# A decoder layer on one core: Q's bias ahead of the exponentials on ScalarE, and the turned probabilities ahead of the tail's transposes on TensorE

## The reference

```
q, k, v = x @ Wq + bq, x @ Wk + bk, x @ Wv + bv      # 16 query heads, 4 key/value heads, 128 wide
q, k    = rope(q), rope(k)
x = layernorm(x + softmax(causal(q @ k.T / sqrt(16))) @ v @ Wo + bo)
x = layernorm(x + wkv(w, u, k=x, v=context))         # a decaying maximum and two decaying sums over the 256 rows
x = layernorm(x + x @ W.T + bias + low_rank_experts(x))   # the 2 best of 16 experts for each row
```

## Time and profile before

| what | value |
|---|---|
| median of 3 runs | 1581.77 us (1580.96 to 1586.83) |
| the profiled execution, its own time | 1579.19 us |
| its span, first to last instruction | 1577.4 us |
| granted TensorE clock, mean | 0.992 |
| busy: PE, PEld, DVE, ACT, POOL | 97%, 89%, 84%, 71%, 64% |

### The profile page before, as it was taken

One profiled execution on the slowest core, in us unless ns is written; L12 is line 12 of the kernel. 1 busy time (PEld: TensorE's weight loads), 2 busy tenths in 40 slices (PEclk: granted clock), 3 DMA queues, 4 the chain that ended last, 5 costly groups with the idle time before them and its releaser, 6 DMA issues.

```text
span 1577.4 us, 32696 instructions
## 1 busy us (share of the span) xinstructions
PE 1534.2 (97%) x10492; PEld 1396.1 (89%) x10492; DVE 1326.1 (84%) x3435; ACT 1117.8 (71%) x2995; POOL 1005.0 (64%) x853
## 2 busy tenths in 40 slices
PE   8999999999999999999999999999999988989998
PEld 7899999999999999999999999999899977878786
DVE  6776688889889888898898989898989897877964
ACT  6877787877787878787878787878787865234333
POOL 2555586757676767676767667676767563644644
PEclk9999999999999999999999999999999998999999
DMA  7776444424441444244424441445144522112121
GB/s 245 243 256 209 156 144 141 129 67 152 148 144 50 154 153 141 62 154 154 141 61 149 142 159 48 125 151 180 48 128 154 167 65 97 58 68 94 60 89 54
DMA packets 81641, 202.62 MB, mean 128 GB/s; under 512 B 10432, under 2 KB 11072, under 8 KB 81472
## 3 DMA queue, kind: packets, MB, share of 16 engines
q1 hardware_dynamic: 81472, 200.53, 40.3%
HBM read 120.80 MB, written 37.75 MB: 101 GB/s over the span
## 4 chain that ended last, share of the span: by engine, by line
PE 81%; DVE 9%; issue 3%; POOL 2%; ACT 2%; DMA 1%; DVEq 1%; SPq 0%; POOLq 0%; ACTq 0%
PE bank L546 24%; PE bank L548 23%; PE bank L547 23%; PE bank L670 5%; PE bank L615 2%; DVE ED L1366 1%; PE bank L616 1%; PE bank L653 1%; PE bank L661 1%; DVE PS L1325 1%; DMA SW<-QB 1%; PE bank L685 1%; DVE OTl L1269 1%; ACT Xh L768 0%; DVE RO L1280 0%
## 5 line engine op out<-in xcount | busy, mean ns | idle before, releaser
L546 PE MATMUL bank<-Xh,W 128*128 128x256 f32 x1280 | 357.4, 279 | 3.6 <-DVE Vl L1242 1.5
L548 PE MATMUL bank<-Xh,W 128*128 128x256 f32 x1280 | 356.2, 278 | 0.0
L547 PE MATMUL bank<-Xl,W 128*128 128x256 f32 x1280 | 355.8, 278 | 0.0
L1050 POOL TENSOR_TENSOR Ql<-RC,Qh 128x512 fp32r<-128x512 f32 x127 | 168.8, 1329 | 191.9 <-ACT Qh L768 191.7
L783 ACT ACTIVATE S<-S,NM 128x128 f32<-128x128 f32 (+1 forms) x512 | 229.0, 450 | 68.7 <-DVE NM L1181 67.7
L1038 POOL TENSOR_TENSOR SW<-SW,tables 128x512 f32<-128x512 f32 x128 | 175.4, 1370 | 125.0 <-DMA SW<-QB 125.0
L546 PEld LDWEIGHTS bank<-Xh,W 128*128 128x128 f32 x1280 | 241.5, 189 | 5.5 <-issue 2.8
L548 PEld LDWEIGHTS bank<-Xh,W 128*128 128x128 f32 x1280 | 241.2, 188 | 0.0
L547 PEld LDWEIGHTS bank<-Xl,W 128*128 128x128 f32 x1280 | 241.0, 188 | 0.0
L768 ACT ACTIVATE PTh<-bank 128x384 fp32r<-128x384 f32 x256 | 125.1, 489 | 148.7 <-PE bank L670 147.6
L768 ACT ACTIVATE S<-S,RL 128x128 f32<-128x128 f32 (+1 forms) x512 | 204.4, 450 | 31.7 <-DVE RL L1188 31.3
(11 more groups left out here) (161 smaller groups left out, 4428.1 us busy)
## 6 DMA issues: line engine op xcount, KB each, us to landing
W<-kept SPq DMA_DIRECT2D x140, 512.0 KB, 4.5
SW<-QB SPq DMA_DIRECT2D x256, 128.0 KB, 2.3
kept<-W SPq DMA_DIRECT2D x40, 512.0 KB, 4.8
XR<-XR SPq DMA_DIRECT2D x64, 128.0 KB, 2.3
RO<-in_xn SPq DMA_DIRECT2D x16, 512.0 KB, 4.0
KVT<-in_ctxt SPq DMA_DIRECT2D x16, 512.0 KB, 4.8
mixed<-RO SPq DMA_DIRECT2D x16, 512.0 KB, 4.5
XR<-in_xt SPq DMA_DIRECT2D x15, 512.0 KB, 4.2
```

What stands on the lines that cost most here:

```text
L546: nc.tensor.matmul(dst, lhs[0], rhs[0], start=first, stop=False)
L547: nc.tensor.matmul(dst, lhs[0], rhs[1], start=False, stop=False)
L548: return nc.tensor.matmul(dst, lhs[1], rhs[0], start=False, stop=last)
L1050: gp.tensor_tensor(Q[1][:, :, :], RC[:, i % 2, :, :], Q[0][:, :, :], ALU.subtract).then_inc(q_lo, 1)
```

## The change

Two calls are moved, one on each of two engines. No instruction is added or taken away.

On TensorE, the turning of the probabilities moves ahead of the tail's transposes. This matters only in the slots that have a piece of the tail: four of every sixteen.

On ScalarE, in odd slots, `before_rotation(n)` moves ahead of `exponentials(n)`. Even slots are as they were.

```diff
@@ TensorE, slot(n), behind the output projection
+                g = head_of(n, L_T)
+                if g is not None:
+                    pe.wait_ge(normed, g + 1)
+                    above(pe, pt_lo, g)
+                    if g == 0:
+                        pe.wait_ge(const_in, 16)
+                    for k in range(3):
+                        last = nc.tensor.transpose(pt_ps[:, k * P:(k + 1) * P], S[:, g % 2, k * P:(k + 1) * P], Ident[:, :])
+                    last.then_inc(turned, 1)
                 for t in range(TT):
                     tau = tail_of(n, T_TURN + t)
...
                         last.then_inc(y_turned, 1)
-                g = head_of(n, L_T)
-                if g is not None:
-                    pe.wait_ge(normed, g + 1)
...
-                    last.then_inc(turned, 1)
@@ ScalarE, odd(n)
                 tail(n, 0)
+                before_rotation(n)
                 exponentials(n)
-                before_rotation(n)
                 extras(n)
                 x_high(n)
```

## The result

| | median | range of runs |
|---|---|---|
| before | 1580.96 us | 1579.02 to 1586.83, 7 runs |
| changed | 1572.34 us | 1571.93 to 1574.44, 6 of 7 runs |

The ratio is 0.9945 with an interval of 0.9934 to 0.9956. That is 8.6 us less, and under the low end of the range, 1574. In a second series of five rounds the changed kernel took 1573.47 us against 1580.91, ratio 0.995 (0.9937 to 0.9963). The seventh run of the changed kernel, the profiled one, was disturbed (1886 us at a granted clock of 0.75), so I read two later profiles, with spans of 1570.2 us both.

The account below looks back on a forecast made before the run. TensorE was taken as the bound, busy 1167.82 of 1170 us from 100 to 1270 us. Savings of 2.2 + 0.2 = 2.4 us took the median 1581.77 us to 1579.4 us; range 1574 to 1585 us.

Parts of the forecast that it names:

- the ceiling: TensorE, 100 to 1270 us: busy 1167.82 of 1170 us, so other engines' order can give back at most 2.2 us.
- the four stalls: TensorE's second half of `y` (L661) waits four times for VectorE's sum L1377: 2.3 us together, 2.2 us saved.
- the 0.2 us at the end: End of the attention, TensorE's waits at L661 and L653: between 0 and 0.7 us saved, 0.2 taken, VectorE being the bound.
- the bias ahead in the other odd slots: ScalarE, Q's bias before the exponentials away from the stalled places: zero, up to 0.3 us a slot without cover.
- the probabilities ahead at `x1`: TensorE's probabilities' transposes ahead of the tail's where nothing waits: priced at nothing, 0.35 us each without the 5.0 us cover.
- The scores of the following slot: TensorE, what would be late next after the stalls vanish; none of the six listed waits is theirs.
- RC comes when it came: VectorE's cosines: it waits longer for the exponentials and less for the bias, so `RC` is not moved; zero.
- TensorE never waited for it here, so nothing: SyncE and GpSimd: the swap starts 0.6 to 0.9 us earlier in odd slots and `Ql` comes earlier; worth nothing.
- The new wait of the bias for the projection: ScalarE, odd slots: the bias ahead may wait 0 to about 0.3 us for TensorE's projection, hidden by 3.0 us of cover.
- the faster rival: Around 1293.29 us, an earlier swap frees VectorE from GpSimd, saving 7.4 us and more: 1574 us; 5%.
- The stall stays: Rival: L1297 is held by GpSimd's L1038 until the same moment, so 1.4 us or nothing saved: 1580.4 to 1581.8 us; 25%.
- The slower rival: Slot 140 and its like, 14 times: an earlier swap puts GpSimd's L1038 before VectorE's scan; 1585 to 1597.5 us; 8%.

## Why the prediction was wrong

**The step that failed is the ceiling.** "... the other engines' order can give back at most what is left: 1170 less 1167.82, 2.2 us." The room was 5.8 to 8.8 us in waits, and more in pace, because a busy matmul row can stand for an engine that waits 0.17 us or runs slower. With the ceiling everything outside the four stalls was priced at zero but for the 0.2 us at the end, and it was there that about three quarters of the gain lay. Two terms of the sum show it: the bias ahead in the other odd slots, put at zero, gave 0.9975, and the probabilities ahead at `x1`, put at nothing, 0.9986. Put right, by the profiles, the sum of 9.2 us would be, but for rounding, 2.2 us for the stalls, 3.3 us for the other waits (1.3 in slots 7, 0.7 in slots 14, 1.3 in slots 0, 1, 2 and 12), 1.6 us for pace, and 2.2 us outside the stretch, of which 1.1 lies between 57 and 92 us. The last two terms, 3.8 of 9.2 us, are measured and not explained.

**The four stalls** were right, in place, mechanism and size: 2.3 us forecast, 2.2 measured, and all of it gone. The end of slot 98 in the changed kernel:

```profile
492.31 0.39 PE L548 MATMUL bank<-W,OTl 128*128 128x512 f32 x1
492.54 0.49 PE L654 MATMUL bank<-tables,S 128*128 128x128 f32 x3
492.87 0.60 PE L670 MATMUL bank<-tables,E2Z 128*128 128x128 f32 x4
```

L670 starts 0.56 us behind the output projection's last matmul; 0.6 was the forecast. But "what is late next? The scores of the following slot; no wait of theirs is among the six" was wrong: late next, and late before, are the cosines in slots 7 and 14 mod 16. Whether the stalls' 2.2 us would have been kept without the rest of the change is not shown: the kernel with the sum ahead points neither way.

**"RC comes when it came"** was wrong, by a part of the path that I didn't price: ScalarE, SyncE, GpSimd, and from there by the lock to VectorE's scans, 0.4 us of VectorE in the mean of 14 places. I had seen that GpSimd's wait for the swap would shrink, and written "TensorE never waited for it here, so nothing". It fell from 89.9 us in 62 waits to this:

```profile
POOL SW L1038 <- DMA SW<-QB: 40.8, 27, 4.0
...
DVE RC L1196 <- ACT QB L801: 36.3, 46, 0.9
DVE RL L1188 <- ACT S L783: 28.1, 40, 1.5
...
ACT QB L801 <- PE bank L548: 12.4, 44, 0.6
```

**VectorE's waits.** I forecast that it would wait longer for the exponentials and less for the bias. The first fell from 33.8 us to 28.1, the second stayed at 36 us in 46 waits where there were 60. So the exchange on ScalarE is not the only thing that moved.

**The new wait of the bias for the projection** was right: 44 times, 12.4 us, 0.28 us each in the mean, within 0 to 0.3, and 0.6 us at most. No listed wait of TensorE lies behind it.

**The end of the attention.** The waits at L661 and L653 are gone; in their place TensorE waits 0.64 us for VectorE's L1269, so the bound is VectorE, as said. 0.2 us forecast; the whole part behind the stretch is 0.7 us shorter in the mean, within the 1.7 us by which three profiles of before differ there. The long idle time stays, 3.26 us for 3.27, so the faster rival had the right sign and the wrong place.

**The rivals.** "The stall stays" was false: L1297 is held as before, 1.25 us, but starts 0.4 us sooner against TensorE's list. The slower rival is real as a mechanism, but its place is cheaper with the change than before it (1.4 us in the mean against 2.1), because the kernel before had the collision too, at a near tie. The one profile that I forecast from had the least of it of three, 0.8 us, which is chance; its slots 92, 156 and 220, where L1038 starts less than 0.03 us behind the scan, were the warning. The mirror image in slot 6 mod 16 was not among the rivals.

## What to carry to other kernels

Don't take the ceiling of an engine from its busy time where rows overlap: measure the distances between starts, and look for first matmuls with 0.39 us in place of 0.28. Price an edit that brings a whole path forward by all the places on that path, not by the listed wait it was found at: here the bias was worth nothing that could be measured in the slots of that wait, and 3.9 us in the others. Where a change moves a GpSimd instruction, check the VectorE instructions on both sides of it: those it will now hold, and those it held until now. Where two of them start within 0.02 us of each other in one profile, take a second one before you price either order.

## What was unexpected of the hardware

The matmuls of 256 columns have two paces in the same list. In slot 53, with no wait and a granted clock of 1.00, the kernel before and the changed one:

```profile
268.09 0.28 PE L548 MATMUL bank<-Xh,W 128*128 128x256 f32 x1
268.21 0.28 PE L546 MATMUL bank<-Xh,W 128*128 128x256 f32 x1
268.33 0.28 PE L547 MATMUL bank<-Xl,W 128*128 128x256 f32 x1
268.45 0.28 PE L548 MATMUL bank<-Xh,W 128*128 128x256 f32 x1
```

```profile
265.08 0.28 PE L548 MATMUL bank<-Xh,W 128*128 128x256 f32 x1
265.19 0.28 PE L546 MATMUL bank<-Xh,W 128*128 128x256 f32 x1
265.31 0.28 PE L547 MATMUL bank<-Xl,W 128*128 128x256 f32 x1
265.42 0.28 PE L548 MATMUL bank<-Xh,W 128*128 128x256 f32 x1
```

Three steps take 0.36 us in one and 0.34 in the other: 0.118 and 0.1135 us each. The distances fall into two heaps with little between. The slow pace begins most often at a slot's scores and lasts for many matmuls. In the stretch the kernel before has 1655, 1622 and 1716 such slow steps, the changed one 1510 and 1461; the kernels with the bias ahead in all odd slots or in slots 5 alone, or with the turning ahead, have 1511 to 1554, the one with the bias ahead everywhere but slots 5 has 1715. So it goes with the order of the other engines' work. Fewer waits often go with fewer slow steps, but not always: with the turning ahead at `y` alone the pace costs as little as in the changed kernel, beside 6.1 us of waits. What sets it I haven't found; its 1.6 us of the gain are measured and not explained.
